# Layer-0 attention of a two-layer transformer: zero-padded keys for the score matmuls, row sums added up on VectorE

## The reference

```python
h = layernorm(x) * (1 + ca) + sa
q = (h @ Wq)  # 16 heads of 64
k = (h @ Wk); v = (h @ Wv)  # 4 key/value heads of 64, each for 4 query heads
q, k = apply_rope(q), apply_rope(k)
scores = einsum('bkgqd,bkpd->bkgqp', q, k) * 64 ** -0.5
probs = softmax(where(causal, scores, -1e30))
x = x + ga * (einsum('bkgqp,bkpd->bkgqd', probs, v) @ Wo)
```

## Time and profile before

| | |
|---|---|
| median of 3 runs | 2068.57 us (2066.3 to 2070.35) |
| profiled execution | 2066.3 us, of which span 2064.2 us |
| PE matmul busy | 1803.1 us (87%) |
| PE weight loads busy | 1320.1 us (64%) |
| DVE busy | 1145.4 us (55%) |
| ACT busy | 690.3 us (33%) |
| POOL busy | 743.9 us (36%) |
| mean granted TensorE clock | 0.957 of full speed |
| chain that ended last | PE 50%, DVE 13%, issue 6%, ACT 2% |

### The profile page before, as it was taken

The page is one execution under the profiler, slowest core; times in us unless marked ns, Lnnn a source line. Parts: engine busy times, 40 slices in busy tenths (PEclk is TensorE's granted clock), DMA queues, the critical chain, the costliest instruction groups (busy, mean ns, idle before and its releaser), DMA issues.

```text
span 2064.2 us, 76401 instructions
## 1 busy us (share of the span) xinstructions
PE 1803.1 (87%) x34864; PEld 1320.1 (64%) x34864; DVE 1145.4 (55%) x2282; ACT 690.3 (33%) x1041; POOL 743.9 (36%) x727
## 2 busy tenths in 40 slices
PE   6899999999888888899999898978888887977994
PEld 4666766766666666575524666766666666756883
DVE  4656666566666665674265555645565545544224
ACT  2333434334333333333101342323333332323431
POOL 2464655555545551311030323313132232014442
PEclk9999999999999999999998999999999989989997
DMA  9500000000000000300012313222131313024666
GB/s 310 164 2 2 2 2 2 2 2 2 2 2 2 2 2 2 103 1 1 3 31 46 82 29 82 52 56 68 38 78 38 73 34 79 20 62 130 198 206 185
DMA packets 81042, 113.45 MB, mean 55 GB/s; under 512 B 9486, under 2 KB 63506, under 8 KB 80289
## 3 DMA queue, kind: packets, MB, share of 16 engines
q1 hardware_dynamic: 71376, 97.16, 17.6%
q0 software_dynamic: 4544, 8.54, 1.2%
q10 hardware_dynamic: 4800, 2.89, 0.6%
HBM read 83.25 MB, written 45.68 MB: 62 GB/s over the span
## 4 chain that ended last, share of the span: by engine, by line
PE 50%; DVE 13%; issue 6%; ACT 2%; DMA 1%; POOL 1%; another core or an unknown queue 1%; POOLq 0%; DVEq 0%; SPq 0%; ACTq 0%
PE psum L1090 47%; DVE colmax L1819 2%; DVE colmax L1972 2%; DVE ctx_sum L1831 1%; PE psum L1438 1%; DVE rowmax L1980 1%; DMA arena<-in_pack 1%; ACT arena L1575 1%; DVE rowmax L1826 1%; DVE arena L1792 1%; DVE stats L1779 1%; DVE raw L1807 1%; PE psum L1165 1%; PE psum L1157 1%
## 5 line engine op out<-in xcount | busy, mean ns | idle before, releaser
L1090 PE MATMUL psum<-arena 128*32 128x32 f32 (+9 forms) x10680 | 679.2, 256 | 84.2 <-issue 56.9
L1090 PEld LDWEIGHTS psum<-arena 128*32 128x32 f32 (+4 forms) x10680 | 489.2, 127 | 205.0 <-issue 128.4
L1575 ACT ACTIVATE arena<-psum 128x1024 f32<-128x1024 f32 (+1 forms) x192 | 169.4, 882 | 359.3 <-PE psum L1090 291.7
L1090 PE MATMUL psum<-prob,ffw 128*32 128x128 f32 x5120 | 206.4, 280 | 40.4 <-DVE rowmax L1826 37.6
L1090 PE MATMUL psum<-neg_ident,rowmax 128*32 128x128 bf16 (+3 forms) x4352 | 215.9, 252 | 11.4 <-issue 10.3
L1972 DVE TENSOR_REDUCE colmax<-psum 128x256 bf16<-128x768 f32 (+2 forms) x160 | 178.3, 1114 | 82.4 <-PE psum L1090 59.3
L1819 DVE TENSOR_REDUCE colmax<-psum 128x512 bf16<-128x2048 f32 (+2 forms) x96 | 168.4, 1755 | 74.7 <-PE psum L1090 74.6
L1980 DVE TENSOR_REDUCE rowmax<-psum 128x2 bf16<-128x256 f32 (+1 forms) x192 | 98.0, 510 | 189.9 <-PE psum L1090 181.3
L1590 ACT COPY ctx_sum<-psum 128x384 f32<-128x384 f32 x128 | 61.2, 478 | 412.4 <-PE psum L1090 366.1
L1090 PEld LDWEIGHTS psum<-prob,ffw 128*32 128x32 f32 x5120 | 139.6, 112 | 71.7 <-DVE rowmax L1826 60.1
L2209 POOL TENSOR_TENSOR arena<-ctx_sum 128x256 f32<-128x256 f32 x128 | 95.4, 745 | 243.9 <-DVE ctx_sum L1831 233.2
(11 more groups left out here) (260 smaller groups left out, 2530.3 us busy)
## 6 DMA issues: line engine op xcount, KB each, us to landing
arena<-in_pack SPq DMA_DIRECT2D x39, 578.0 KB
sent<-in_empty SPq DMA_DIRECT2D x9, 2112.0 KB, 34.7
arena<-qk_parts SPq DMA_DIRECT2D x96, 128.0 KB
q_copies<-arena SPq DMA_DIRECT2D x32, 256.0 KB, 3.9
prob<-q_copies SPq DMA_DIRECT2D x128, 64.0 KB, 3.6
qk_parts<-arena SPq DMA_DIRECT2D x16, 384.0 KB, 3.8
arena<-sent SPq DMA_DIRECT2D x39, 132.0 KB
ffw<-in_L_w SPq DMA_DIRECT2D x1, 2048.0 KB, 9.0
```

Source lines behind the costliest of these rows:

```text
L1090: return pe.matmul(o, lhsT, rhs, start=start, stop=stop, skip_group_check=True)
L1575: act.activation(probs_of(i)[:, :, h0 * P:(h0 + nh) * P], slot(n)[:, 0:(i + 1) * W].rearrange("p (j c) -> p j c", c=W), ACT.Exp, scale=HD1 ...
```

## The change

It does four things in layer 0's attention, and leaves the other phases as they are.

- The rotated keys are stored twice, in `k_pad[0]` with the partitions 64 to 127 zero and in `k_pad[1]` with 0 to 63 zero. Each key rotation on GpSimd ends in two additions on 64 partitions instead of one on 128. The zeros are written once for each of the two buffers (`memset`: two at the start, two in a new step `constant_parts` in unit 2 of batch 0). Score matmuls contract over all 128 partitions with queries of both head pairs; their number and their 256 columns stay.
- Scores of one key tile now fill one PSUM bank, [key tile, 4 heads x 128]. The causal mask is one matmul of 512 columns. A unit takes i + 1 banks. The reduction, the exp and the copy read the same number of elements in the new order.
- The shift is one matmul of 128 columns for each key tile and head: 16, 12, 8, 4 for i = 3, 2, 1, 0 (before: 8, 8, 4, 4).
- The row sums: a new step `sums` for units with i > 0, after `maxima` of n + 1 and ahead of `scores` of n + 2, has VectorE add the probabilities of unit n - 1 over its key tiles into `prob_sum`: for i = 3 one addition of 1024 columns and one of 512, for i = 2 two of 512, for i = 1 one of 512. Then only four ones matmuls are left for each unit, at the end of `values`, behind a wait for `summed`.

```diff
-        kT = [carve([KP, S]), kq[:, 0, 0:KP * S].rearrange("p (m s) -> p m s", m=KP)]
+        k_pad = [[carve([KP, S]), kq[:, par, 0:KP * S].rearrange("p (m s) -> p m s", m=KP)] for par in range(2)]
+        prob_sum = carve([2, BANK])
...
         def scores_of(u):
-            i, k0 = u["i"], u["k0"]
-            banks = 1 + i // 2
-            a = psum[:, k0:k0 + 2 * banks, :].rearrange("p (z k) c -> p z (k c)", z=2)[:, :, 0:(i + 1) * 2 * P]
-            return a.rearrange("p z (j c) -> p z j c", c=2 * P)
+            return psum[:, u["k0"]:u["k0"] + u["i"] + 1, :]
 
         def prob_of(u):
-            a = prob[:, u["n"] % 2, 0:(u["i"] + 1) * BANK]
-            return a.rearrange("p (z j c) -> p z j c", z=2, c=2 * P)
+            return prob[:, u["n"] % 2, 0:(u["i"] + 1) * BANK].rearrange("p (j c) -> p j c", c=BANK)
...
-                n_pool = (4 if what == "key" else 5 + QC) if L else 1
+                n_pool = (4 if what == "key" else 5 + QC) if L else (2 if what == "key" else 1)
...
+            def sums(u):
+                if u["i"]:
+                    sum_of[u["n"]] = add("sums", u=u)
...
                     add("maxima", u=st[n + 1])
+                if n:
+                    sums(st[n - 1])
                 if n + 2 < len(st):
                     scores(st[n + 2])
...
                 late_side.setdefault(n, []).append(prepare_steps[b][Q0 + 3])
+                late_side.setdefault(n + 2, []).append(lambda: add("constant_parts", pool=2))
...
                         for j in range(i + 1):
                             for par in range(2):
-                                rows = slice(HD0 * par, HD0 * (par + 1))
-                                mm(scores_of(u)[:, par, j, :].rearrange("p (a q) -> p a q", a=2),
-                                   kT[z][rows, m, j * P:(j + 1) * P], qT[z][rows, 2 * q:2 * q + 2, i * P:(i + 1) * P],
-                                   start=(j % 2 == 0))
+                                mm(scores_of(u)[:, j, 256 * par:256 * (par + 1)].rearrange("p (a q) -> p a q", a=2),
+                                   k_pad[par][z][:, m, j * P:(j + 1) * P],
+                                   qT[z][:, 2 * q:2 * q + 2, i * P:(i + 1) * P], start=(par == 0))
                         w.wait_ge(consts_ready, 1)
-                        for par in range(2):
-                            ins = mm(scores_of(u)[:, par, i, :], ident_bf[:, :],
-                                     causal[:, :].unsqueeze(1).to_broadcast([P, 2, P]), False)
-                        ins.then_inc(scored, 1)
+                        mm(scores_of(u)[:, i, :], ident_bf[:, :],
+                           causal[:, :].unsqueeze(1).to_broadcast([P, GRP, P]), False).then_inc(scored, 1)
...
                         w.wait_ge(max0_done, n + 1)
-                        for h in range(GRP):
-                            par, a = divmod(h, 2)
-                            for j in range(0, i + 1, 2):
-                                nj = min(2, i + 1 - j)
-                                ins = mm(scores_of(u)[:, par, j:j + nj, a * P:(a + 1) * P],
-                                         rowmax[:, n % 2, h:h + 1].to_broadcast([P, P]),
-                                         neg_ident[:, :].unsqueeze(1).to_broadcast([P, nj, P]), False)
+                        for j in range(i + 1):
+                            for h in range(GRP):
+                                ins = mm(scores_of(u)[:, j, h * P:(h + 1) * P],
+                                         rowmax[:, n % 2, h:h + 1].to_broadcast([P, P]), neg_ident[:, :], False)
...
                         for j in range(i + 1):
-                            for c in range(3):
+                            for c in range(2):
                                 for h in range(GRP):
                                     d0 = HD0 * (2 * m + h // 2) + QUAD * c
-                                    ins = mm(psum[QUAD * h:QUAD * (h + 1), CTX, c * P:(c + 1) * P],
-                                             v0[b % 2][:, j, d0:d0 + QUAD] if c < 2 else ones_col[:, :],
-                                             prob_of(u)[:, h // 2, j, h % 2 * P:(h % 2 + 1) * P], start=(j + c == 0))
+                                    mm(psum[QUAD * h:QUAD * (h + 1), CTX, c * P:(c + 1) * P],
+                                       v0[b % 2][:, j, d0:d0 + QUAD], prob_of(u)[:, j, h * P:(h + 1) * P],
+                                       start=(j + c == 0))
+                        if i:
+                            w.wait_ge(summed, sum_of[n].n + 1)
+                        for h in range(GRP):
+                            ins = mm(psum[QUAD * h:QUAD * (h + 1), CTX, 2 * P:CW], ones_col[:, :],
+                                     (prob_sum[:, 0, :] if i else prob_of(u)[:, 0, :])[:, h * P:(h + 1) * P], start=False)
...
+                    elif k == "sums":
+                        u = s["u"]
+                        i, n = u["i"], u["n"]
+                        w.wait_ge(prob_ready, n + 1)
+                        w.wait_ge(ctx_full, n)
+                        if i == 3:
+                            chain.mark(dve.tensor_tensor(prob_sum, prob_of(u)[:, 0:2, :], prob_of(u)[:, 2:4, :], ALU.add))
+                            chain.wait()
+                            ins = dve.tensor_tensor(prob_sum[:, 0, :], prob_sum[:, 0, :], prob_sum[:, 1, :], ALU.add)
+                        elif i == 2:
+                            chain.mark(dve.tensor_tensor(prob_sum[:, 0, :], prob_of(u)[:, 0, :], prob_of(u)[:, 1, :],
+                                                         ALU.add))
+                            chain.wait()
+                            ins = dve.tensor_tensor(prob_sum[:, 0, :], prob_sum[:, 0, :], prob_of(u)[:, 2, :], ALU.add)
+                        else:
+                            ins = dve.tensor_tensor(prob_sum[:, 0, :], prob_of(u)[:, 0, :], prob_of(u)[:, 1, :], ALU.add)
+                        ins.then_inc(summed, 1)
...
+                for par in range(2):
+                    chain.wait()
+                    chain.mark(pool.memset(k_pad[par][0][HD0 * (1 - par):HD0 * (2 - par), :, :], 0.0))
...
                             if what == "key":
-                                chain.wait()
-                                chain.mark(pool.tensor_tensor(kT[b % 2][:, i, :], rope_a[:, z, :], raw[:, z, :], ALU.add))
+                                for par in range(2):
+                                    rows = slice(HD0 * par, HD0 * (par + 1))
+                                    chain.wait()
+                                    chain.mark(pool.tensor_tensor(k_pad[par][b % 2][rows, i, :], rope_a[rows, z, :],
+                                                                  raw[rows, z, :], ALU.add))
```

More of the change, by code:

```diff
@@ L471, in band_slice @@
             return band[:, e0:e0 + P]
-        order = Order(pool=1)
+        order = Order(pool=3)
         add = order.add
@@ L478, in build @@
         projected, rotated, value_of, out_of, routed, late_of, late_at = {}, {}, {}, {}, {}, {}, {}
-        cm_at, cm_counts = {}, {"v": 0, "a": 0}
+        cm_at, cm_counts, sum_of = {}, {"v": 0, "a": 0}, {}
         units = []
@@ L590, in attention @@
                     f()
+            sums(st[-1])
             add("values", u=st[-1])
@@ L904, in build @@
         v_constants = [s for s in order.steps if s.kind == "v_constants"][0]
-        POOL_KINDS = ("stat", "project", "rotated", "late", "split_prob", "before_gather",
+        POOL_KINDS = ("constant_parts", "stat", "project", "rotated", "late", "split_prob", "before_gather",
                       "v_constants", "q_zero")
@@ L936, in build @@
             semaphore(n) for n in ("x_full", "x_loaded", "moments_ready", "normed", "rot_a", "swapped", "key_rest"))
+        summed = semaphore("summed")
         scored, colmax_dve, colmax_act, max0_full, max0_done, shifted, prob_ready, ctx_full, ctx_drained, recip = (
@@ L1550, in _ @@
                         w.wait_ge(scored, n + 1)
-                        act.copy(colmax[:, n % 2, :].rearrange("p (z c) -> p z c", z=2),
-                                 scores_of(u)[:, :, 0, :]).then_inc(colmax_act, 1)
+                        act.copy(colmax[:, n % 2, :], scores_of(u)[:, 0, :]).then_inc(colmax_act, 1)
                     elif k == "exp":
@@ L1557, in _ @@
                         w.wait_ge(shifted, n + 1)
-                        act.activation(prob_of(u).rearrange("p z j c -> p z (j c)"),
-                                       scores_of(u).rearrange("p z j c -> p z (j c)"), ACT.Exp,
-                                       scale=HD0 ** -0.5).then_inc(prob_ready, 1)
+                        act.activation(prob_of(u), scores_of(u), ACT.Exp, scale=HD0 ** -0.5).then_inc(prob_ready, 1)
                     elif k == "scores1" and s["u"]["i"] == 0:
@@ L1818, in _ @@
                             w.wait_ge(scored, n + 1)
-                            dve.tensor_reduce(colmax[:, n % 2, :].rearrange("p (z c) -> p z c", z=2),
```

(6 more changed lines are left out.)

## The result

The changed kernel takes 2167.47 us (median of 4, 2164.66 to 2167.8) against 2069.46 us: a ratio of 1.0474, 95% interval 1.0457 to 1.0492, so 98 us slower. The forecast was 2164 us, with a range of 2112 to 2193.

The account below looks back on a forecast made before the run. The prediction took TensorE's own instruction stream to bound the layer-0 attention phase. Stream 67, covered waits -13, column maximum 4 and additions 40 sum to 98 us on 2066.3, thus 2164 us, range 2112 to 2193.

Parts of the forecast that it names:

- the likeliest case: Whole kernel: longer TensorE stream and mostly exposed VectorE additions make it slower, 2164 us; chance 0.65.
- Price of a full-row f32 matmul, 0.43: Layer-0 attention scores: padded matmuls run one after the other at 0.43 us each, +3.70 us a group of four units.
- Rival 3: Scores: not slower, because full-row matmuls cost only 0.217 us each; time 2028 us; chance 0.03.
- Bare weight loads: Scores: the full-row matmuls' weight loads come into the open, 243 us more, about 2400 us; chance 0.02.
- Stream, +67: TensorE in layer-0 attention: scores, operand changes, shifts and saved ones matmuls together add 2.10 us a group, +67 us.
- Covered waits, -13: TensorE's waits for VectorE's row maximum: longer scores cover a third of the 37.6 us, -13 us.
- Column maximum, +4: TensorE's waits for the column maximum: shorter values cover less of it, so these waits grow by 4 us.
- Additions, +40: VectorE's row-sum additions: collisions with GpSimd end them after the values matmuls, so TensorE waits, +40 us (4 to 53).
- GpSimd's key additions, 0: Key rotations: two 64-partition additions add 1.28 us 16 times, hidden in GpSimd's idle time, 0 us.
- Rival 1: VectorE's additions hide, only 4 us of their waits staying; time 2128 us; chance 0.22.
- Rival 2: VectorE and GpSimd become the pace, delays carry over, 1.3 us more a group; time 2206 us; chance 0.08.

Follow-up runs that it names:

- e3: Kernel before with padded keys alone (two key copies, split key additions, 128-row score matmuls), old bank layout, shifts and ones matmuls kept: 2159.26 us against 2067.73, ratio 1.0444.
- e1: Changed kernel without VectorE's additions, row sums again by ones matmuls for each key tile: 2158.14 us, ratio 1.0442.
- e4: Changed kernel with the additions left out, its four ones matmuls a unit reading only key tile 0: 2125.31 us, ratio 1.0278.
- e7: Kernel before with only GpSimd's part: two key copies, zero fills, split key additions; scores still contract over 64 rows: ratio 1.0070.
- e2: Kernel before with VectorE's additions and four ones matmuls a unit, keys unpadded, old layout: 2092.96 us, ratio 1.0116.
- e6: Kernel before with part of the row sums on VectorE: one addition for each unit with i > 0, remaining sums by ones matmuls: ratio 1.0039.
- e8: Kernel before with one VectorE addition of 512 columns for units i = 1 and i = 2, units i = 3 untouched: ratio 1.0036.

## Why the prediction was right, step by step

The size came out within 4 us, and the likeliest case with it. Its terms did less well than the sum: errors of 5 to 7 us in both directions cancel, so that the last few us are luck. Measured values are distances of the second table.

- *Price of a full-row f32 matmul, 0.43.* Shown: 0.435 (3.56, 2.70, 1.78 and 0.96 a group, 9.00 in all instead of 8.84), and by e3 that padding alone brings it. Two matmuls on 64 rows each had run side by side: 0.43 a pair. Rival 3 is out.
- *Bare weight loads.* Out as well: the step holds two matmuls in 0.87 while their four loads of 0.19 run beside them. The sentence of the Trainium skill by which loads overlap running matmuls only when the row group differs ("TensorE: Matmul & The Clock Gate", Part 3, The mechanism) isn't what e3 and the changed kernel show. The same section also lets a load into the background weight buffer run ahead, which would fit.
- *Stream, +67.* Too low by some 10. The scores cost 123.0 instead of 118. At the start of the scores 6.7 is saved instead of 12. The ones matmuls saved are 42.1 as forecast (e1 against e4). The lower bound is also added up wrongly: without the 0.06 four times a group it is +60 and not +62.
- *Covered waits, -13.* Too small. The row maximum's list fell by 11.3, the distance by 18.2, and without the additions (e4) by 19.7.
- *Column maximum, +4.* Its list grew by 8.6. Without the additions (e4) the list has +4.0 and the distance +7.6; the additions bring a further 4.1.
- *Additions, +40.* By e4 they cost 40.1, all effects together: 30.7 at the ones matmuls, of which the list has 21.6, and the rest further on. The place was right, the detail in part. The prediction laid waits on three of four groups, 5.9 us a batch at A; the batch shown has them in two, 2.5 us by the list (in the phase 17 of the 32 units A wait). The order of the collision is as forecast in the first and fourth groups, and wrong in the second: GpSimd's power operation doesn't hold VectorE up, and a pair of the two that overlaps freely is shown at the end, against "nothing of such a pair overlaps". What the prediction put at nothing, the delays further on, makes most of the other 9. That the total is the forecast's 40 is luck.
- *GpSimd's key additions, 0.* This step failed for the kernel before: e7 measures 0.45 to 0.95%. "On an engine with 42 us of idle time and needed units later" looked at who needs the key, and not at VectorE's swap, which is queued behind it and ahead of the row maximum. How much of it is left under the long scores of the changed kernel wasn't measured by itself; it is contained in e3's 92.
- *The clock.* The prediction has no term for it. The kernel before has a granted clock of 0.98, 0.98 and 0.95 in the windows 534 to 634, 634 to 734 and 734 to 830 us, the changed one 1.00, 1.00 and 0.98. An estimate from the clock records of both phases (23.8 us at 1.2 GHz before, 10.2 after, each losing at most half): the change may have got back up to 7 us.
- *Rival 1* (2128) is out by e4: with the additions gone altogether the ratio is still 1.0278, and they cost 40. *Rival 2* is out for the changed kernel (107.6 a batch). What it describes, delays that carry over to the row and column maxima, is what e2 shows without the padding.

My expectations of the runs were worse than the forecast. e2, e6 and e8 came out 0.4 to 1.2% slower than before where I had expected a gain, all for one reason: saved TensorE time was counted in full, and the row and column maxima behind VectorE's longer queue at too little. In the unpadded kernel that queue is nearly as tight as TensorE's.

## What to carry to other kernels

Here two f32 matmuls over 64 rows each, one after the other in different halves of the array, took the time of one (0.43 us a pair, 0.87 when padded); look at the distance of starts before padding them to 128 rows. Add up distances of starts, not only listed waits, before you call a cost small: the list had 21.6 of 30.7 us. Work moved from TensorE to VectorE is worth what is left after its place in the queue: find what stands behind it (here the row maximum) and what runs on GpSimd at that moment, because two dependent additions with two SBUF inputs can each wait for a GpSimd operation (2.27 instead of 1.22 us, 1.63 instead of 0.69). An addition on an engine with idle time isn't free if another engine's swap, in the path, is queued behind it (e7: 9 to 19 us).

## What the runs showed of the hardware

- A VectorE reduction over four blocks of 512 f32 in SBUF takes 3.78 us, out of PSUM 2.29; for three blocks 1.90 against 1.76, for two 1.22 in both. The ones out of SBUF write float32, the ones out of PSUM bfloat16; which of the two differences makes it was not tried.
- GpSimd's power operation on 128x4 doesn't exclude VectorE's addition for its whole length. In one place the addition starts 0.35 us into it, and neither is longer than alone:

```profile
84.02 1.05 POOL L2175 TENSOR_TENSOR rstd<-moments,minus_half 128x4 f32<-128x4 f32 x1
84.37 1.21 DVE L1835 TENSOR_TENSOR arena<-prob 128x1024 f32<-128x1024 f32 x1
```

  In six others both start within 0.02 us, the power operation takes 2.13 and the addition 1.22. Which was first can't be told from so small a distance, since spans on GpSimd are rough. The Trainium skill ("SBUF — State Buffer", SBUF: two separate sides) gives the ports to whoever starts first, for the whole instruction. The multiplies follow that (2.27 and 2.12 us above), the pair at 84.02 doesn't.
- The kernel before took 1997 us on one chip and 2068 to 2072 on the others. The phase behind layer 0's attention is 1235.7 us in its profile and 1166.6 in e7's, on the faster chip. TensorE's idle time put down to "issue" ahead of one group of its layer-1 matmuls (4608 records) is 44.5 us and 13.1. The granted clock differs too: 0.957 against 0.975 in these two profiles. At most this makes 4.3% of 2064 and 2.5% of 2001 us, 89 and 50, so up to 39 of the 69 us (an estimate). What makes either was not tried; it is why each run is read by its ratio.
